# A two-direction GRU on one core: the state scan with three columns an image instead of four, its factor scaled on GpSimd

## What is computed

```
gh = h @ whh.T + bhh
xr, xz, xn = split(xt); hr, hz, hn = split(gh)
r = sigmoid(xr + hr)
z = sigmoid(xz + hz)
n = tanh(xn + r * hn)
h_new = (1.0 - z) * n + z * h
```

## Time and profile before

| | before |
|---|---|
| time, median of 3 runs | 1904.64 us (1901.84 to 1905.37) |
| profiled execution, time | 1902.69 us |
| profiled execution, span | 1900.9 us |
| PE busy / PEld busy | 86% / 66% |
| DVE busy | 84% |
| ACT busy | 65% |
| POOL busy | 3% (58.1 us) |
| granted tensor clock, mean | 0.516 of full speed |

### The profile page before, as it was taken

The page is one execution under the profiler, slowest core; times in us unless marked ns, Lnnn a source line. Parts: engine busy times, 40 slices in busy tenths (PEclk is TensorE's granted clock), DMA queues, the critical chain, the costliest instruction groups (busy, mean ns, idle before and its releaser), DMA issues.

```text
span 1900.9 us, 65131 instructions
## 1 busy us (share of the span) xinstructions
PE 1639.2 (86%) x21315; PEld 1248.0 (66%) x21315; DVE 1602.0 (84%) x9056; ACT 1226.8 (65%) x6271; POOL 58.1 (3%) x131
## 2 busy tenths in 40 slices
PE   3558989898989989898998999898988999898987
PEld 2336666666666666666666666666666666666665
DVE  7788888888888888888888888888888888888887
ACT  7935666666666666666666666666666666666665
POOL 4420000000000000000000000000000000000000
PEclk9655555555555555555555555555555555555555
DMA  4200000000000000000000000000000000000000
GB/s 152 67 7 10 11 13 11 13 10 14 11 12 12 11 13 11 14 10 13 11 13 5 12 12 12 12 12 12 10 13 11 12 12 12 12 12 12 10 13 13
DMA packets 40133, 31.27 MB, mean 16 GB/s; under 512 B 3449, under 2 KB 37625, under 8 KB 39801
## 3 DMA queue, kind: packets, MB, share of 16 engines
q1 hardware_dynamic: 39800, 27.13, 4.9%
HBM read 18.73 MB, written 8.39 MB: 14 GB/s over the span
## 4 chain that ended last, share of the span: by engine, by line
PE 68%; DVE 16%; ACT 9%; issue 6%; DMA 0%; DVEq 0%; POOL 0%; SPq 0%; ACTq 0%; POOLq 0%
PE bank L592 67%; DVE bank L875 5%; DVE state L887 4%; ACT rec L496 3%; ACT rpair L490 3%; DVE halves L896 3%; DVE big L866 1%; ACT big L432 1%; ACT zquad L493 1%; DVE rec L902 1%; ACT seq L428 1%; DMA gamma_row<-in_gamma 0%; DVE stats L721 0%; DVE seq L850 0%; DVEq L886 0%
## 5 line engine op out<-in xcount | busy, mean ns | idle before, releaser
L592 PEld LDWEIGHTS bank<-halves,wsplit 128*128 128x128 f16 x18432 | 726.7, 107 | 535.1 <-DVE halves L896 386.7
L592 PE MATMUL bank<-halves,wsplit 128*128 128x16 f16 x18432 | 876.9, 182 | 187.2 <-DVE halves L896 185.1
L887 DVE TENSOR_TENSOR_SCAN state<-zquad,rec 128x64 f32<-128x64 f32 x2048 | 597.2, 292 | 180.4 <-ACT rec L496 134.2
L490 ACT ACTIVATE rpair<-bank 128x16 f32<-128x16 f32 x2048 | 380.5, 186 | 337.7 <-PE bank L592 319.7
L592 PE MATMUL bank<-seq,wcomb 128*128 128x128 f32 x1536 | 593.0, 491 | 0.4 <-DVE seq L850 0.4
L496 ACT ACTIVATE rec<-bank 128x16 f32<-128x16 f32 x2048 | 406.3, 198 | 284.1 <-DVE bank L875 82.3
L875 DVE TENSOR_TENSOR_SCAN bank<-rpair,bank 128x32 f32<-128x32 f32 x2048 | 445.6, 218 | 49.4 <-ACT rpair L490 25.0
L896 DVE SCALAR_TENSOR_TENSOR halves<-state 128x32 f16<-128x32 f32 x2048 | 430.6, 210 | 34.8
L493 ACT ACTIVATE zquad<-bank 128x16 f32<-128x16 f32 x2048 | 406.7, 199 | 19.8
L592 PEld LDWEIGHTS bank<-seq,wcomb 128*128 128x128 f32 x1536 | 385.9, 312 | 1.3 <-DVE seq L850 1.3
L902 DVE TENSOR_TENSOR rec<-state,signs 128x32 f32<-128x32 f32 x2047 | 372.8, 182 | 3.1
(11 more groups left out here) (118 smaller groups left out, 203.5 us busy)
## 6 DMA issues: line engine op xcount, KB each, us to landing
xin<-in_x SPq DMA_DIRECT2D x16, 512.0 KB, 3.7
big<-in_x SPq DMA_DIRECT2D x128, 64.0 KB
out<-big SPq DMA_DIRECT2D x128, 64.0 KB
wih<-in_wiht SPq DMA_DIRECT2D x2, 384.0 KB
con<-in_consts SPq DMA_DIRECT2D x1, 424.0 KB, 5.2
whh<-in_whht SPq DMA_DIRECT2D x2, 192.0 KB
inw<-in_in_w SPq DMA_DIRECT2D x1, 128.0 KB
outw<-in_outwt SPq DMA_DIRECT2D x2, 64.0 KB
```

What stands on the lines that cost most here:

```text
L490: act.activation(rpair[:, e, 2 * B * d:2 * B * (d + 1)].rearrange("p (n k) -> p n k", k=2)[:, :, 1], R[q][:, at:at + B], ACT.Sigmoid, scal ...
L592: return nc.tensor.matmul(o, w, m, start=start, stop=True, skip_group_check=True)
L887: v.tensor_tensor_scan(state[:, d, ring, :], zquad[:, e, cols], rec[:, e, cols], 0.0, ALU.mult, ALU.add).then_inc(state_ready[d], 1)
```

## The change

The state is kept with three columns an image. The factors are now (0, K(1-z), 1) in `gain`, the addends (-n, (1-z-1)*K*h, -BIG) in `drive`, and the scan subtracts the addend: out[i] = factor[i] * out[i-1] - addend[i] yields n, then K(1-z)n + z*K*h = K*h_new, then the same plus BIG. The tanh has a negative scale so that it gives -n. ScalarE writes the update sigmoid (1-z) into `keep`. From `keep`, GpSimd computes the middle factor K(1-z) with a tensor_scalar of 16 columns (`scaled_gain`, one for each step and direction, 2048 in all), and VectorE the middle addend with a scalar_tensor_tensor of 16 columns (`hold_state`), (keep - 1) times the old state. `hold_state` belongs to the step it serves: it stands before its own state scan, at the two places in `body` where a record stood, and waits for the update sigmoid of its own turn. The state scan waits for the tanh, for GpSimd's factor and for the hold. Setup on GpSimd fills 11 constants in place of 15.

```diff
--- before.py
+++ after.py
@@ -165,12 +165,12 @@
     diag = sb("diag", [B, B])
     mask = sb("mask", [P, B], I32)
 
-    state = sb("state", [P, 2, RING + 1, 4 * B])
-    rec = sb("rec", [P, 2, 4 * COLS])
-    signs = sb("signs", [P, 2 * COLS])
+    state = sb("state", [P, 2, RING + 1, 3 * B])
+    drive = sb("drive", [P, 2, 3 * COLS])
     halves = sb("halves", [P, 2, 2, 2, B], F16)
     rpair = sb("rpair", [P, 2, 2 * COLS])
-    zquad = sb("zquad", [P, 2, 4 * COLS])
+    keep = sb("keep", [P, 2, COLS])
+    gain = sb("gain", [P, 2, 3 * COLS])
 
 
     bank = [ctx.enter_context(nc.psum_tensor(f"bank{i}", [P, 512], F32)) for i in range(8)]
@@ -228,7 +228,8 @@
     cand_ready = [sem(f"cand_ready{d}") for d in range(2)]
     state_ready = [sem(f"state_ready{d}") for d in range(2)]
     halves_ready = [sem(f"halves_ready{d}") for d in range(2)]
-    rec_ready = [sem(f"rec_ready{d}") for d in range(2)]
+    gain_ready = [sem(f"gain_ready{d}") for d in range(2)]
+    drive_ready = [sem(f"drive_ready{d}") for d in range(2)]
     square_set = sem("square_set")
     norm_mm = sem("norm_mm")
     norm_set = sem("norm_set")
@@ -259,7 +260,11 @@
 
     def state_of(r, d):
 
-        return state[:, d, r // TB * TB + place(r % TB, d), :].rearrange("p (n k) -> p n k", k=4)
+        return state[:, d, r // TB * TB + place(r % TB, d), :].rearrange("p (n k) -> p n k", k=3)
+
+    def thirds_of(t, e, d):
+
+        return t[:, e, 3 * B * d:3 * B * (d + 1)].rearrange("p (n k) -> p n k", k=3)
 
     block = ctx.enter_context(nc.Block())
 
@@ -331,23 +336,19 @@
                     sp.dma_start(tile_rows(out_tok, kk), tiles[:, kk, :]).then_inc(out_done, 16)
         sp.wait_ge(out_done, 16 * NBLK)
 
-    N_INIT = 15
+    N_INIT = 11
 
     @block.gpsimd
     def _(g):
 
         g.memset(rpair[:, :, :], 0.0).then_inc(init_done, 1)
         for e in range(2):
-            quad = zquad[:, e, :].rearrange("p (n k) -> p n k", k=4)
-            g.memset(quad[:, :, 0], 0.0).then_inc(init_done, 1)
-            g.memset(quad[:, :, 1], K).then_inc(init_done, 1)
-            g.memset(quad[:, :, 3], 1.0).then_inc(init_done, 1)
-            rows = rec[:, e, :].rearrange("p (n k) -> p n k", k=4)
-            g.memset(rows[:, :, 1:3], 0.0).then_inc(init_done, 1)
-            g.memset(rows[:, :, 3], BIG).then_inc(init_done, 1)
-        pairs = signs[:, :].rearrange("p (n k) -> p n k", k=2)
-        g.memset(pairs[:, :, 0], -1.0).then_inc(init_done, 1)
-        g.memset(pairs[:, :, 1], 1.0).then_inc(init_done, 1)
+            thirds = gain[:, e, :].rearrange("p (n k) -> p n k", k=3)
+            g.memset(thirds[:, :, 0], 0.0).then_inc(init_done, 1)
+            g.memset(thirds[:, :, 2], 1.0).then_inc(init_done, 1)
+            thirds = drive[:, e, :].rearrange("p (n k) -> p n k", k=3)
+            g.memset(thirds[:, :, 1], 0.0).then_inc(init_done, 1)
+            g.memset(thirds[:, :, 2], -BIG).then_inc(init_done, 1)
         g.memset(halves[:, :, :, :, :], 0.0).then_inc(init_done, 1)
         g.memset(state[:, :, RING, :], 0.0).then_inc(init_done, 1)
 
@@ -401,6 +402,16 @@
         g.tensor_scalar(parts[2], parts[0], -1.0, None, ALU.mult)
         g.tensor_tensor(parts[1], w_all, parts[0], ALU.subtract).then_inc(weights_set, 1)
 
+        def scaled_gain(turn, d):
+            e = (turn - 1) % 2
+            g.wait_ge(update_ready[d], turn)
+            g.tensor_scalar(thirds_of(gain, e, d)[:, :, 1], keep[:, e, B * d:B * (d + 1)], K, None,
+                            ALU.mult).then_inc(gain_ready[d], 1)
+
+        for turn in range(1, L + 1):
+            for d in range(2):
+                scaled_gain(turn, d)
+
 
     @block.scalar
     def _(act):
@@ -490,12 +501,12 @@
                     act.activation(rpair[:, e, 2 * B * d:2 * B * (d + 1)].rearrange("p (n k) -> p n k", k=2)[:, :, 1],
                                    R[q][:, at:at + B], ACT.Sigmoid, scale=inverse).then_inc(reset_ready[d], 1)
                     act.wait_ge(update_pre[d], turn)
-                    act.activation(zquad[:, e, 4 * B * d:4 * B * (d + 1)].rearrange("p (n k) -> p n k", k=4)[:, :, 2],
+                    act.activation(keep[:, e, B * d:B * (d + 1)],
                                    Z[q][:, at:at + B], ACT.Sigmoid, scale=negative).then_inc(update_ready[d], 1)
                     act.wait_ge(cand_pre[d], turn)
-                    act.activation(rec[:, e, 4 * B * d:4 * B * (d + 1)].rearrange("p (n k) -> p n k", k=4)[:, :, 0],
+                    act.activation(thirds_of(drive, e, d)[:, :, 0],
                                    cand[:, (2 * e + d) * 2 * B:(2 * e + d + 1) * 2 * B].rearrange("p (n k) -> p n k", k=2)[:, :, 1],
-                                   ACT.Tanh, scale=inverse).then_inc(cand_ready[d], 1)
+                                   ACT.Tanh, scale=negative).then_inc(cand_ready[d], 1)
 
         def recurrence(inverse, negative):
             for i in range(L // RING):
@@ -621,7 +632,7 @@
...
         def project(q, d):
 
-            h = state[:, d, q * TB:(q + 1) * TB, :].rearrange("p s (b k) -> p (s b) k", k=4)[:, :, 2]
+            h = state[:, d, q * TB:(q + 1) * TB, :].rearrange("p s (b k) -> p (s b) k", k=3)[:, :, 1]
             return mm(Y[:, d * C:(d + 1) * C], h, outw[:, d, :], start=(d == 0))
 
         def output_bias():
@@ -877,39 +888,39 @@
                                  ALU.mult, ALU.add).then_inc(cand_pre[d], 1)
 
         def new_state(base, r, d):
-            e, cols = r % 2, slice(4 * B * d, 4 * B * (d + 1))
+            e, cols = r % 2, slice(3 * B * d, 3 * B * (d + 1))
             ring = r // TB * TB + place(r % TB, d)
             turn = base + (r + 1)
             dve.wait_ge(cand_ready[d], turn)
-            dve.wait_ge(update_ready[d], turn)
-            if not (isinstance(base, int) and base + r == 0):
-                dve.wait_ge(rec_ready[d], base + r)
-            v.tensor_tensor_scan(state[:, d, ring, :], zquad[:, e, cols], rec[:, e, cols], 0.0,
-                                 ALU.mult, ALU.add).then_inc(state_ready[d], 1)
+            dve.wait_ge(gain_ready[d], turn)
+            if turn > 1:
+                dve.wait_ge(drive_ready[d], turn - 1)
+            v.tensor_tensor_scan(state[:, d, ring, :], gain[:, e, cols], drive[:, e, cols], 0.0,
+                                 ALU.mult, ALU.subtract).then_inc(state_ready[d], 1)
 
         def split_state(base, r, d):
             e = r % 2
             new = state_of(r, d)
             dve.wait_ge(state_ready[d], base + (r + 1))
             slot = r // TB * TB + place(r % TB, d)
-            both = state[:, d, slot::RING - slot, 2::4]
-            v.scalar_tensor_tensor(out=halves[:, e, d, :, :], in0=new[:, :, 3].unsqueeze(1).to_broadcast([P, 2, B]),
+            both = state[:, d, slot::RING - slot, 1::3]
+            v.scalar_tensor_tensor(out=halves[:, e, d, :, :], in0=new[:, :, 2].unsqueeze(1).to_broadcast([P, 2, B]),
                                    scalar=-BIG, in1=both, op0=ALU.add, op1=ALU.subtract).then_inc(halves_ready[d], 1)
 
-        def record_state(r, d):
+        def hold_state(base, r, d):
             e = r % 2
-            new = state_of(r, d)
-            v.tensor_tensor(rec[:, 1 - e, 4 * B * d:4 * B * (d + 1)].rearrange("p (n k) -> p n k", k=4)[:, :, 1:3],
-                            new[:, :, 2:3].to_broadcast([P, B, 2]),
-                            signs[:, 0:2 * B].rearrange("p (n k) -> p n k", k=2), ALU.mult).then_inc(rec_ready[d], 1)
+            old = state_of((r - 1) % RING, d)
+            dve.wait_ge(update_ready[d], base + (r + 1))
+            v.scalar_tensor_tensor(out=thirds_of(drive, e, d)[:, :, 1], in0=keep[:, e, B * d:B * (d + 1)], scalar=-1.0,
+                                   in1=old[:, :, 1], op0=ALU.add, op1=ALU.mult).then_inc(drive_ready[d], 1)
 
         def body(base, kblk, first):
             share = (L - 2 * EDGE) // RING
             for r in range(RING):
                 q, s = r // TB, r % TB
                 candidate(base, r, 0)
-                if not (first and r == 0):
-                    record_state((r - 1) % RING, 1)
+                if base + r > 0:
+                    hold_state(base, r, 0)
                 if s in (3, 5) and kblk + q > 0:
                     add_output(kblk + q - 1, s // 4)
                 if first:
@@ -919,7 +930,8 @@
                 new_state(base, r, 0)
                 candidate(base, r, 1)
                 split_state(base, r, 0)
-                record_state(r, 0)
+                if base + r > 0:
+                    hold_state(base, r, 1)
                 new_state(base, r, 1)
                 split_state(base, r, 1)
 
```

## The result

The changed kernel takes 1917.69 us (median of 4 runs, 1916.33 to 1923.02), the kernel before 1904.72 us beside it: ratio 1.0076, with a 95% interval of 1.0054 to 1.0099. It is 13 us slower; against the kernel before as it ran beside the later experiments (medians 1901.5 to 1902.4 us) it is 15 to 16. The forecast had said slower by 67 us. The profiled execution took 1923.02 us with a span of 1921.2, and 3.7 us of its distance to the profile before lie ahead of the recurrence: its first state scan starts at 124.4 us, that of the kernel before at 120.7.

The account below looks back on a forecast made before the run. A chain of dependent small instructions was taken to bound five turns of eight: 5 x 128 x 0.105 = 67 us on the median 1904.64 gives 1972 us. The likeliest case's range was 1940 to 2045, the wide range 1872 to 2045.

Parts of the forecast that it names:

- same: Whole kernel: time within 0.2% (4 us) of before; chance 0.07.
- What bounds the kernel: Five turns of eight: a chain of dependent small instructions, 1.62 us; the other three: the tensor engine.
- GpSimd's path: Between z and state scan: longer than what it replaces, 0.46 us for 0.37 (d0) and 0.32 (d1); chance 0.58.
- X: From z to state scan: hand-over to GpSimd, its instruction, hand-over to VectorE; 0.46 us, bounds 0.42 and 0.55.
- The worth of three columns: State scan, 64 to 48 columns: 0.035 us shorter, on both directions' cycles; 22 us if counted in five turns.
- I leave them too: Bias-matmul turns of 1.80 and 1.75 us: unchanged, like the 2.07 us projection turn.
- uses that up: Bias-matmul turns: d1 is held up about 0.2 us, and a later d1 consumes that wait.
- The turn takes the longer cycle: Two directions sharing in-order queues: d1's +0.105 us sets the turn, not d0's +0.055; 1.62 becomes 1.725 us.
- The hold at nothing: VectorE's 16-column hold replacing the record: no cost; if it starts late, the scan slips at most 0.18 us.
- The gain: Rival: GpSimd's part hidden under candidate and tanh, X at most 0.355 us on d1; 1874 to 1882 us; chance 0.19.
- The port fight: Rival: GpSimd's scaling held until VectorE's hold is over, X 0.61 us, about 2080 us; chance 0.14 in full.
- The tensor engine as the only bound: Rival: neither scan nor GpSimd counts much and the time stays; chance 0.09 together with balance.

Follow-up runs that it names:

- run 3: Run 1 with a hold that reads the state alone, a step ahead, the product z*h left out: 1850.6 us, ratio 0.973.
- run 4: The kernel before, four columns and record kept, with the sigmoid's result passed through GpSimd (times 1): 1964.3 us, ratio 1.032.
- run 1: The changed kernel with K = 1 and no GpSimd scaling, ScalarE writing 1-z where the scan reads it: 1877.4 us, ratio 0.9863.
- run 7: The changed kernel with the projection reading a constant tile in 16-byte steps, projected values left out: 1924.33 us, ratio 1.0112.
- run 9: The changed kernel with GpSimd's multiplication done twice, the first into an unused tile: 2203.97 us, ratio 1.1587.
- runs 5 and 6: The changed kernel with K = 1 and GpSimd for one direction only: direction 1 alone 1913.58 us (1.0054), direction 0 alone 1892.35 us (0.9952).
- run 2: Run 1 with the state scan no longer waiting for z itself, as the hold already did: 1859.26 us, ratio 0.9776.

## Why the prediction was right in direction and wrong in size

1917.69 us lies in none of the prediction's cases: it is below the forecast's own range (1940 to 2045) and above the 0.2% of "same", a stretch to which it gave 0.02. That the wide range, 1872 to 2045, contains it is luck, since that range only spans from the gain to the forecast's upper bound.

**What bounds the kernel: right.** A turn is a chain of small dependent instructions, and every experiment that moved a link of it moved the turn. The tensor engine alone is not the limit: run 3 has the same matmuls, only the projection's 17 ns shorter each (9 us in all), and takes 52 us less.

**GpSimd's path: right in sum, by parts that cancelled.** X was forecast as 0.17 + 0.24 + 0.05 = 0.46. Measured in direction 1 it is 0.082 to GpSimd's start, 0.28 for the instruction and 0.088 to the scan, 0.45. The hand-over in was put too high; why the setup's row is longer (GpSimd had been idle 7.02 us there, 0.6 here) stays open. The hand-over out was put too low: 0.05 is from the split to the matmuls, and the scan takes GpSimd's signal through a separate wait instruction. Alone the step costs 62 us (run 4).

**The worth of three columns: the term that was mis-sized.** The prediction gave it 0.035 us in five turns of eight, 22 us. Without the two new dependences it is 52 us (run 3). The table has its parts: 0.06 us in each plain turn (0.31 a block), 0.05 in the projection turn, 0.04 in the two bias turns. In a plain turn direction 1's state scan starts 0.024 earlier behind direction 0's than before, since the candidate scan queued between them starts 0.033 earlier; its own scan is 0.034 shorter; so direction 0's next candidate scan, queued behind it, starts 0.06 earlier. The scan's gain counts in both directions, and the prediction counted it once.

Minus 52 and plus 62 make plus 10, near the 13, but times of this kind need not add: in run 1 the hold that waits for z costs 27 us, and GpSimd's step on top of it 40, so the same way from run 3 to the changed kernel is 67 us.

**"I leave them too": the step that failed.** The prediction let the tensor-bound turns stand at 2.07, 1.80 and 1.75. They fell by 0.19 us together, 24 us over the kernel. Some of it is the projection reading the state in steps of 12 bytes (0.076, run 7). The rest is cover, that is, time for which direction 1 waited anyway. In the kernel before, direction 1's state scan stands 0.68 us behind direction 0's in a plain turn (1012.53 to 1013.21), but 0.85 in turn 3, because its matmuls wait there for a fill:

```profile
1005.06 0.60 PE L592 MATMUL bank<-ind,bias 6*128 6x256 bf16 x1
1005.12 0.21 DVE L896 SCALAR_TENSOR_TENSOR halves<-state 128x32 f16<-128x32 f32 x1
...
1005.59 0.41 PE L592 MATMUL bank<-halves,wsplit 128*128 128x16 f16 x9
...
1006.59 0.29 DVE L887 TENSOR_TENSOR_SCAN state<-zquad,rec 128x64 f32<-128x64 f32 x1
```

The split ends at 1005.33 and its matmuls start at 1005.59, where 0.06 was enough in the earlier trace rows. In the changed kernel direction 1's scan stands 0.80 behind in a plain turn already (1008.38 to 1009.18), and what it lost there it need not lose again. The traces show the cover itself: the time from the end of direction 1's split to its next reset sigmoid (median, us) is 0.34 where nothing is in the way, and longer after four of the eight turns:

| split of turn | before | after | GpSimd step alone (run 4) | GpSimd twice (run 9) |
|---|---|---|---|---|
| 0 | 0.61 | 0.51 | 0.54 | 0.34 |
| 2 | 0.54 | 0.42 | 0.44 | 0.34 |
| 3 | 0.50 | 0.47 | 0.44 | 0.34 |
| 7 | 0.55 | 0.39 | 0.45 | 0.34 |

A later direction 1 waits less for the tensor engine, and in run 9, where it is later still, it waits no more. Run 4 shows what that is worth without the three columns: the three tensor-bound turns fall by 0.07 together. So the prediction's sentence that a later direction 1 "uses that up" was right, but it does not follow that the turn stays: the delay before it is paid in the plain turns and given back here. For the same reason turn 1, which follows the projection and begins with a small lag again (0.73, from turn 2 on 0.80), pays 0.02 and not 0.10.

**The turn takes the longer cycle: right only when the lag has built up,** which runs 5 and 6 show by 36 us against 15. In turns 2, 5, 6 and 7 it held, with +0.07 and not +0.105: from z to the scan direction 1 needed 0.13 us more (0.14 forecast), and its cycle had lost 0.034 by the scan as forecast, but also 0.015 by the sigmoid and 0.013 by the split.

The account of the 67 us: five plain turns at 0.105 should have been four at 0.072 and one at 0.023, -27 us; the projection turn -15; the bias turns -9. That leaves 16, by the table, and 13 by the runs.

**The hold at nothing: right in the plain turn, not everywhere.** In the timeline of the changed kernel direction 1's hold ends at 1008.96 (1008.79 and 0.17), 0.22 us before the scan at 1009.18. In turns 1, 3 and 4 the hold is the last to come, 0.132 before the scan, though only some 0.01 us later than GpSimd's signal would allow. It becomes the bound of direction 1 in every turn as soon as GpSimd's step goes (0.132 before the scan): 27 us in run 1.

**The rivals.** The gain did not come, since X was never near 0.355 (its lower end is 1873 by its own terms, not 1874). The port fight exists and is small. Alone GpSimd's multiplication takes 0.26 us. In the turn shown direction 1's starts 0.02 after its hold and takes 0.28, and in other turns up to 0.32, or the hold takes 0.21 in place of 0.17. These 0.02 us and more are inside the 0.45 on direction 1's path; at 0.02 in the four plain turns from turn 2 on that is 10 us by estimate, most of the slowdown, and no run takes it away by itself. The Trainium skill (SBUF — State Buffer, Who interferes with whom) says that the later of two such instructions is fully blocked. In the plain turns the trace does not agree: behind the hold GpSimd would end 0.26 us after it, and it ends 0.13 after it. Beside a long VectorE instruction it does agree, as in the earlier trace rows: in each of the first turns VectorE also copies 960 columns under a mask, and direction 1's multiplication ends 0.09 after that instruction:

```profile
140.38 1.22 DVE L861 COPY_PREDICATED seq<-mask,big 128x960 f32<-128x960 int32 x1
...
141.09 0.60 POOL L408 TENSOR_SCALAR gain<-keep 128x16 f32<-128x16 f32 x1 [0.50 <-ACT keep L504]
```

This costs nothing to speak of, as the first 16 turns take 38.6 us in the changed kernel and 38.7 before. The tensor engine as the only bound is ruled out by runs 3 and 9.

## What to carry to other kernels

When two chains share in-order queues, don't price an edit by one steady turn: list the turns with another bound, and for each ask by how much the lagging chain waits there already, since that wait pays for a delay before it and takes back part of a gain (in run 3, with direction 1 earlier, the wait behind the split of turn 2 grew from 0.54 to 0.57). Write a wait only for what no earlier instruction of the same queue has waited for: one redundant semaphore was worth 18 us of 1877. And before a scaling goes to another engine, ask whether the scale is needed at all: with it at 1 the step could go, and with the redundant wait gone too the loss of 13 us became a gain of 42. What the smaller scale does to the precision of the halves is not measured here.

## What the runs showed of the hardware that was not expected

- A state scan that waits for its tanh alone starts 0.033 us after it. Where the last signal goes through the separate wait instruction it is 0.087 to 0.132 us: 0.132 behind the hold with two semaphores in it (run 1), 0.103 with one (run 2). That instruction takes 50 ns and 21 ns there.
- The step between elements shows in small instructions: the split takes 210 ns at 16 bytes and 192 to 195 at 12, the update sigmoid of 16 columns writes in 199 ns at 16 bytes, 192 at 12 and 184 without gaps, and a projection's matmul reading 12-byte steps takes 496 ns where it took 513.
- A GpSimd tensor_scalar of 16 columns takes 0.26 us, starts 0.08 us after the sigmoid that it waits for, and a second one follows the first after 0.32 us. Beside a short VectorE instruction with two inputs either of the two gets some 0.02 to 0.06 us longer.
